# Two row halves for the similarity matmuls of a product-key layer, and an offset moved from 4096 activations into 128 copies

## The reference, cut to what matters

```
q      = (x @ Wq_pk)                    # 2 x 8 heads x 32
sim    = einsum('pbnhd,pkhd->pbnhk')    # 2 sets of 64 sub-keys, 8 heads: 1024 similarities a token
top 16 of each 64; 16 x 16 sums; the best 16 of them -> softmax -> kv_scores, indices
k, v   = sum over 16 of kv_scores * keys_table[ind], values_table[ind]   # 4096 rows for each head
attn   = softmax(causal(q k^T)); out = attn v @ Wo
```

## Time and profile before

| | |
|---|---|
| time, median of 3 runs | 7143.39 us (7125.44 to 7164.84) |
| profiled execution | 7148.1 us, its span 7146.3 us |
| PE busy | 6374.5 us (89%) |
| ACT busy | 5014.1 us (70%) |
| POOL busy | 4384.9 us (61%) |
| DVE busy | 4028.8 us (56%) |

### The profile page before, as it was taken

How to read it: one execution, slowest core, us unless ns; L and a number is a source line. 1 busy time by engine, 2 the same in 40 slices (tenths; PEclk the granted TensorE clock), 3 DMA queues, 4 the chain that set the end, 5 groups by cost and what they waited for, 6 DMA issues and landing times.

```text
span 7146.3 us, 96532 instructions
## 1 busy us (share of the span) xinstructions
PE 6374.5 (89%) x28800; PEld 3607.7 (50%) x28800; DVE 4028.8 (56%) x13327; ACT 5014.1 (70%) x10873; POOL 4384.9 (61%) x4108
## 2 busy tenths in 40 slices
PE   2799999999999999999999999999999999999967
PEld 1455555555555555555555555555555555555533
DVE  7574747556474654647475464747556474751156
ACT  0677777777777777777777777777777777777722
POOL 0575857667585765758576575857657585767600
PEclk9999999999999999999999999999999999999967
DMA  1111111111111111111111111111111111111100
GB/s 32 45 48 36 50 38 45 44 36 45 35 50 36 42 47 36 45 38 48 38 45 44 36 48 35 51 35 45 47 34 48 38 48 38 45 43 45 40 19 13
DMA packets 93567, 291.74 MB, mean 41 GB/s; under 512 B 17879, under 2 KB 26546, under 8 KB 92780
## 3 DMA queue, kind: packets, MB, share of 16 engines
q1 hardware_dynamic: 92748, 285.25, 12.2%
q10 hardware_dynamic: 288, 0.07, 0.0%
HBM read 280.68 MB, written 4.61 MB: 40 GB/s over the span
## 4 chain that ended last, share of the span: by engine, by line
PE 70%; POOL 10%; ACT 9%; DVE 6%; issue 5%; DVEq 0%; ACTq 0%; DMA 0%; SPq 0%
PE accu L519 29%; POOL dense_w L451 10%; PE dense L526 8%; PE dense L505 8%; PE dense L507 7%; PE sims L637 3%; PE work L643 2%; ACT past L909 1%; PE work L630 1%; PE work L565 1%; PE sims L607 1%; PE work L683 1%; PE dense L491 1%; PE work L617 1%; ACT dense_w L904 1%
## 5 line engine op out<-in xcount | busy, mean ns | idle before, releaser
L451 POOL TENSOR_TENSOR dense_w<-dense_w,store 128x375 f32<-128x375 f32 x4096 | 4382.6, 1083 | 2402.6 <-ACT dense_w L904 2322.8
L519 PE MATMUL accu<-dense_w,store 128*128 128x375 f32 x8192 | 3316.3, 488 | 145.1 <-POOL dense_w L451 83.5
L909 ACT ACTIVATE past<-dense,edge 128x375 bf16<-128x375 f32 x4096 | 2351.4, 574 | 862.4 <-PE dense L526 838.5
L904 ACT ACTIVATE dense_w<-dense 128x375 f32<-128x375 f32 x4096 | 1953.8, 477 | 174.0 <-PE dense L507 170.4
L519 PEld LDWEIGHTS accu<-dense_w,store 128*128 128x128 f32 x8192 | 1424.2, 192 | 470.3 <-POOL dense_w L451 216.8
L526 PE MATMUL dense<-store,hot 128*128 128x375 bf16 x4096 | 1337.0, 326 | 134.1 <-ACT past L909 133.3
L505 PE MATMUL dense<-store,spread 96*128 96x375 bf16 x4096 | 1346.8, 329 | 27.0 <-ACT dense_w L904 26.8
L507 PE MATMUL dense<-past,far 128*128 128x375 bf16 x4096 | 1341.1, 327 | 0.0
L526 PEld LDWEIGHTS dense<-store,hot 128*128 128x128 bf16 x4096 | 398.1, 97 | 1232.9 <-ACT past L909 1084.0
L505 PEld LDWEIGHTS dense<-store,spread 96*128 96x128 bf16 x4096 | 401.4, 98 | 518.6 <-issue 310.1
L507 PEld LDWEIGHTS dense<-past,far 128*128 128x128 bf16 x4096 | 408.0, 100 | 228.9 <-issue 19.0
(11 more groups left out here) (254 smaller groups left out, 6447.3 us busy)
## 6 DMA issues: line engine op xcount, KB each, us to landing
store<-in SPq DMA_DIRECT2D x513, 512.0 KB, 3.4
x_in<-in SPq DMA_DIRECT2D x16, 187.5 KB, 2.4
store<-in SPq DMA_DIRECT2D x1, 2048.0 KB, 9.1
queries_kept<-n3T SPq DMA_DIRECT2D x16, 93.8 KB, 3.3
h_saved<-h SPq DMA_DIRECT2D x16, 93.8 KB
store<-queries_kept SPq DMA_DIRECT2D x16, 93.8 KB, 2.3
store<-h_saved SPq DMA_DIRECT2D x16, 93.8 KB
out<-store SPq DMA_DIRECT2D x16, 93.8 KB
```

Of the source, the lines that this page charges most:

```text
L451: nc.gpsimd.tensor_tensor(dense_w[:, i % RING, :], dense_w[:, i % RING, :], first_of[:, i // CHUNKS, :], ALU.mult).then_inc(s["weighed"], 1)
L519: last = mm(accu[:, 0, 0:S], table[:, n % PIECE_RING, i % PIECE, :], dense_w[:, i % RING, :], start=(c == 0), stop=(c == CHUNKS - 1))
L904: fn(dense_w[:, i % RING, :], dense[:, n % 2, 0:S], ACT.Relu).then_inc(s["taken"], 1)
L909: fn(past[:, j % 2, :], coded, ACT.Relu, bias=edge[:, 0:1]).then_inc(s["past"], 1)
```

## The change

`simw` becomes 128 x 512: the 512 columns of the first matmul lie on partitions 0 to 63, those of the second on 64 to 127. `n2T` becomes 128 x 375: the turned tokens are copied twice from PSUM, to either half. The two matmuls of a tile read different halves of the partitions, so they use different row halves of PE. They are as many and as large as before.

The offset of the mask is added when the ranks are copied instead of when the mask is made. DVE sets rows 64 to 127 of `edge` to 0 once, so that -15 stays on the rows of one sub-key alone; the copy of the ranks becomes an Identity activation with `edge` as bias, and the mask a Relu without bias.

```diff
-        simw = sb("simw", [D, 2 * H * SUB])
+        simw = sb("simw", [128, H * SUB])
-        n2T = sb("n2T", [D, S])
+        n2T = sb("n2T", [128, S])
...
                 for c in range(2):
-                    last = mm(sims[0:P, c, :], n2T[:, tile(t)], simw[:, c * 512:(c + 1) * 512], start=True, stop=True)
+                    half = slice(c * D, (c + 1) * D)
+                    last = mm(sims[0:P, c, :], n2T[half, tile(t)], simw[half], start=True, stop=True)
...
-                nc.scalar.copy(n2T_now, n2T[:]).then_inc(s["kept"], 1)
+                nc.scalar.copy(n2T_now, n2T[0:D]).then_inc(s["kept"], 1)
...
                 if k == 0:
-                    last = nc.scalar.copy(ranksT[:, h, :], src)
+                    last = fn(ranksT[:, h, :], src, ACT.Identity, bias=edge[:, 0:1])
...
-                    fn(past[:, j % 2, :], coded, ACT.Relu, bias=edge[:, 0:1]).then_inc(s["past"], 1)
+                    fn(past[:, j % 2, :], coded, ACT.Relu).then_inc(s["past"], 1)
...
-                nc.scalar.copy(n2T[:], work[0:D, 1, 0:S]).then_inc(s["nT_done"], 1)
+                nc.scalar.copy(n2T[0:D], work[0:D, 1, 0:S])
+                nc.scalar.copy(n2T[D:128], work[0:D, 1, 0:S]).then_inc(s["nT_done"], 1)
...
-                    v.tensor_copy(simw[:], sims[0:D].rearrange("p c k -> p (c k)")).then_inc(s["fold_done"], 1)
+                    v.memset(edge[SUB:128], 0.0)
+                    v.tensor_copy(simw[0:D], sims[0:D, 0])
+                    v.tensor_copy(simw[D:128], sims[0:D, 1]).then_inc(s["fold_done"], 1)
```

## The result

The changed kernel takes 7050.64 us (median of 3 runs, 7050.59 to 7056.83) against 7143.39 us. The ratio is 0.9871, with a 95% interval from 0.9827 to 0.9916: 1.3% or 93 us faster, where -50 us was forecast and 7062 us was the low end of the range. The profiled execution took 7056.8 us, its span is 7055.0 us.

A forecast was written before the change was run, and what follows sets the result against it. PE was taken to bound the kernel, with 70% of the chain. The terms -39.4 + 7.4 - 20 + 2 = -50 us gave 7093 us against the median of 7143.4, range 7062 to 7134 us.

The forecast's parts named there:

- Row halves: Line 607, similarities: the two matmuls run paired, 1.13 us instead of 1.95 a tile, 39.4 us saved over 48 tiles.
- Second copy: Line 950, one more copy of the tokens on ACT, PE waiting for it: 16 x 0.46 = 7.4 us lost.
- The mask: Line 909 on ACT without bias, 97 ns shorter each: 20 us saved on the chain, bounds 0 and 45 us.
- the ranks: Line 889 on ACT, 128 copies 0.1 us longer with a bias: 2 us lost, bounds 0 and 13 us.
- a little more: ACT work queued behind a mask starts up to 0.1 us sooner; at most 13 us from 128 accumulator copies.
- No loss downstream: After tile 2, POOL's 27.00 us stretch starts when PE and ACT get there, so earlier tiles shift it; gain passes.
- Its two marks: Slower verdict: 172 us more at 1.2 GHz, mean clock under 0.946; twice today's share: 107 us more, 7200 us.
- Hidden gain: Rival, chance 0.22: at tiles 1 and 2 the 0.82 us are lost to POOL or DVE; -14 us, 7129 us.
- Matmuls in a row: Rival, chance 0.07: line 607's matmuls do not pair; -11 us, 7132 us, or 7112 us with the middle pair alone.
- More from ACT: Rival, chance 0.09: ACT catches up sooner after other work, its upper bound of 45 us comes; -75 us, 7068 us.
- Slower by the clock: Rival, chance 0.05: longer PE idle time at tile 0 makes half clock more frequent; +57 us, 7200 us.
- Slower by table loads: Rival, chance 0.03: Identity outside the loaded table, two 1283 ns loads for each of 128 copies; 328 us at most, 7421 us.

The follow-up runs named there:

- row halves alone: Kernel before with simw, n2T, similarities and both token copies as in the changed kernel, mask and ranks as before: 7102.21 us, ratio 0.991.
- The second copy alone: Kernel before plus the second copy of the turned tokens, whose second half nobody reads: 7178.47 us, ratio 1.0031.
- the padded kernels: Kernel before with similarities over 128 rows, 64 holding zeros: 7125.51 us; the same plus the mask and ranks edit: 7094.63 us.
- the first masks long: Changed kernel with a bias of zeros given back to the first mask of each group of slots on ACT: 7117.31 us, ratio 0.9938.
- tile 0 first: Changed kernel, ACT copying tile 0's 125 columns to both halves before the other 250: 7082.62 us, on another chip 7072.29 us.

## Why the prediction was wrong, point by point

**The sum, -50 us.** At equal clock the runs give -70 us. The terms:

- *Row halves, -39.4.* Right in size, nearly all of it. Line 608 takes 1.13 us for a tile, as worked out from line 555, and the two parts of this edit gave -30 us against -32. The trace of tile 0 shows the pairs: two starts 7 ns apart, then two 36 ns apart. The Trainium skill (TensorE: Matmul & The Clock Gate, Part 3, What overlaps and what doesn't) has matmuls in strict program order. Had both passes of one half come first, 21 us less would have been saved; the paired starts speak against that order.
- *Second copy, +7.4.* Right: +6.5 us.
- *The mask, -20, and the ranks, +2.* The size failed: -36 us together, against -18. The term multiplied line 909's share of the chain, or 144 stalls, by one mask. But a stall in which ACT does other work has a mask at either end: one ahead of that work on ACT's queue, one behind it that PE waits for. The chain showed only the second, since it steps from the other work to whatever released it last. The prediction named the queue as "a little more" and bounded only its accumulator copies, at 13 us. The waits for the mask and the accumulator account for 28 of the 36 us; the other 8 are not placed.
- *No loss downstream.* Right at tile 0, mostly right at tile 1, wrong at tile 2. Medians of the turns, before and with the row halves alone: from tile 0's similarities to tile 1's, at full clock, 57.20 and 56.38 us, the whole 0.82 us; from tile 1's to tile 2's, with one stretch of 3.4 us at half clock, 78.11 and 77.46 us, 0.65 us. From tile 2's to the beginning of POOL's long stretch it is 20.39 and 20.28 us: only 0.11 us of the 0.82 is there. In the changed kernel (from 3286.5 on) POOL is busy for 17.15 of these 20.15 us, and it is line 451 whose share of the chain grew. POOL's long stretch is 27.07 us before and after. What is lost so is under 0.7 us in each turn, some 10 us (an estimate), and the -30 us leave room for only a part of it.

**The step that failed most: the clock.** The sum was made as if the granted clock stayed at 0.970. It rose by 0.007 in the mean of the runs (to 0.973 to 0.977), worth 38 us at 5.5 us for each 0.001. The forecast looked at the place, saw the half clock behind tile 0, and made it a rival with the sign turned round: more idle time, less clock. The second copy alone shows that this half is true at this place (14 of 14 turns, and the mean clock of its runs down by 0.0026, though its profiled execution had 0.972). But the same edit makes the similarities use both halves of PE's rows at once, for a shorter time, and with that it is 1 to 5 turns of 14 instead of 7 or 8.

The rival also priced the clock wrongly. It took a mean of 0.970 for 3% of the span at 1.2 GHz. With only full and half clock it means 6%, and the trace has 428 us, not 214. So 0.001 of the mean is 14 us at half clock and can cost up to 7 us, twice what the prediction had; the runs gave 5.5. Its two marks move with this: 172 us more at half clock is a mean of 0.958, not 0.946, and twice the share of before could cost up to 214 us, not 107.

**What is shown and what stays open.** That full rows instead of half of them, at equal length, remove the half clock behind tile 0 is shown by the padded kernels. Whether in the changed kernel it is the two halves at once or the shorter time that does it there, no run separates. And it is not the whole rise. The profiles have 428 us at half clock before and 360, 370 and 326 us in the changed kernel. Of the 68 us between the first two, 20 are behind tile 0, worth some 10 us; behind tile 1 there are 14 us more (12 turns instead of 8); from tile 2 to the next tile 0, where the start of the attention lies, there are 55 us less (157 and 102), and the other 7 lie outside the loop. This large part moves from kernel to kernel: with the first masks long, row halves and all, it is 170 us, and twelve runs had 0.9677. What decides it there stays open.

**The rivals.** Hidden gain: at tile 2 in the main, as above; at equal clock the sum still came out larger than forecast, so not in its size. Matmuls in a row: no. More from ACT: yes, by its mechanism, 36 of its 45 us. Slower by the clock: its mechanism exists, but the clock of the whole went the other way. Slower by table loads: no, 32 on line 867 as before on 866.

## What to carry to other kernels

Before costing an edit to TensorE, look at the granted clock around the instructions that it touches; here four half-height matmuls between two idle stretches had half clock behind them in 8 of 14 turns, and with full rows in none. Convert a mean clock into time at half clock with care: 1% of mean clock is 2% of the span. Look at the other places too, since the half clock that goes at one can come at the next. When an instruction that recurs in an engine's queue gets shorter, count the stalls of the engine that waits and ask how many of these instructions stand in one stall, in front of the other work as well as behind it; the chain shows one of them only. And compare kernels at the same clock: here twenty runs of one kernel lay 46 us apart, and 44 of these go with the clock by the line.

## What the runs showed of the hardware that was not expected

Filling rows 64 to 127 with zeros made a kernel 32 us faster, though every matmul took as long as before. The instruction behind the last similarity matmul started 0.43 us after it instead of 0.52 us, with 128 rows in it instead of 64. In the changed kernel the half clock behind tile 0 went from 8 turns of 14 to 2 to 4, and behind tile 1 from 8 to 12 or 13. 0.4 us less idle time in each turn (tile 0 first) left the mean clock lower, not higher, than in the changed kernel. A pointer as bias cost ACT about what was forecast, in either direction: the mask went from 574 to 484 ns, the copy of the ranks, a plain copy before, from 470 to 572.
